# A graph kernel's loading stage and first node stage, written as one stage without engine loops

## The reference

```python
x_ij = jnp.concatenate([x[src], x[dst]], axis=1)
m_ij = jax.nn.relu(x_ij @ W.T + b)            # W is 512 x 1024
out = jax.ops.segment_sum(m_ij, src, num_segments=1250)
...
# second layer: attention, scores from h = x @ W1.T per head
e_src = einsum('ehd,hd->eh', h[src], a_src);  e_dst = einsum('ehd,hd->eh', h[dst], a_dst)
e = leaky_relu(e_src + e_dst, 0.2) * (1.0 + et_emb[edge_type]) * edge_weight[:, None]
```

## Time and profile before

| | |
|---|---|
| median of 3 runs | 1908.78 us (1907.65 to 1910.08) |
| the profiled execution | 1905.63 us, of which 1903.9 us are the span from first to last instruction |
| PE busy | 1596.2 us, 84% of the span, at a mean granted clock of 0.931 |
| DVE, ACT, POOL busy | 61%, 24%, 37% of the span |
| loading stage, from SP's first DMA to n0's first DVE instruction | 484.95 to 500.26 us |
| n0, to the first DVE instruction of e0 | 500.26 to 583.42 us |

### The profile page before, as it was taken

How to read it: one execution, slowest core, us unless ns; L and a number is a source line. 1 busy time by engine, 2 the same in 40 slices (tenths; PEclk the granted TensorE clock), 3 DMA queues, 4 the chain that set the end, 5 groups by cost and what they waited for, 6 DMA issues and landing times. The chain is left out here.

```text
span 1903.9 us, 26664 instructions
## 1 busy us (share of the span) xinstructions
PE 1596.2 (84%) x7565; PEld 956.2 (50%) x7566; DVE 1161.4 (61%) x2308; ACT 459.8 (24%) x875; POOL 700.1 (37%) x605
## 2 busy tenths in 40 slices
PE   6556939876698999998788379996698899999998
PEld 6524723335344555554555245553346445864486
DVE  7889959974375777775577766665865722122222
ACT  3101114424013555553344110000110111001100
POOL 0005878874475766640000547775330110000000
PEclk9988969998698999999799589999799999999999
DMA  0056841009315666680496447776005202330033
GB/s 26 1 215 247 286 118 12 3 2 358 133 39 155 209 188 187 187 143 34 176 361 236 133 121 210 210 209 158 2 1 173 70 0 106 138 111 0 1 138 137
DMA packets 76360, 249.16 MB, mean 131 GB/s; under 512 B 14901, under 2 KB 28582, under 8 KB 68346
## 3 DMA queue, kind: packets, MB, share of 16 engines
q1 hardware_dynamic: 38618, 147.08, 21.2%
q0 software_dynamic: 34592, 96.87, 19.0%
q10 hardware_dynamic: 3072, 4.20, 0.8%
HBM read 215.93 MB, written 32.00 MB: 130 GB/s over the span
## 5 line engine op out<-in xcount | busy, mean ns | idle before, releaser
L659 POOL DMA_INDIRECT tab_slots<-slot_words,slot_address x160 | 232.4, 1452 | 219.7 <-issue 209.0
L688 POOL DMA_INDIRECT e_rows<-tab_h,idx_h x176 | 178.7, 1015 | 290.5 <-POOLq L50 217.3
L1431 PE MATMUL dense_pY<-weights,dense_xT_block 128*128 128x512 f32 x640 | 284.0, 601 | 0.0
L1479 PE MATMUL dense_pY<-parts,dense_number 128*128 128x512 f32 x1000 | 237.2, 398 | 5.7 <-DMA dense_number<-tab_edges_to 5.7
L982 POOL DMA_INDIRECT e_rows<-tab_q,idx_q x192 | 182.0, 948 | 99.8 <-PE e_pS L1055 38.8
L1479 PEld LDWEIGHTS dense_pY<-parts,dense_number 128*128 128x128 f32 x1000 | 188.3, 189 | 53.3 <-DMA dense_number<-tab_edges_to 6.4
L782 PE MATMUL e_pS<-e_rows,e_onehot_ring 128*128 128x512 f32 x352 | 193.8, 641 | 21.7 <-DVE e_rows L758 18.6
L1431 PEld LDWEIGHTS dense_pY<-weights,dense_xT_block 128*128 128x128 f32 x640 | 121.5, 193 | 143.3 <-issue 143.3
L1055 PE MATMUL e_pS<-e_rows,e_onehot_f 128*128 128x512 f32 x384 | 181.6, 596 | 0.0
L867 PE MATMUL count_pA<-count_onehot_d,count_onehot_s 128*128 128x512 f16 (+1 forms) x576 | 132.4, 352 | 42.0 <-DVE count_onehot_d L850 40.9
L758 DVE TENSOR_TENSOR e_rows<-e_rows,e_pW 128x1024 f32<-128x1024 f32 x88 | 107.3, 1220 | 68.6 <-DMA e_rows<-tab_h,idx_h 68.5
(11 more groups left out here) (310 smaller groups left out, 2393.5 us busy)
## 6 DMA issues: line engine op xcount, KB each, us to landing
basis_piece<-in_L_gnn_basis_pieces SPq DMA_DIRECT2D x32, 2048.0 KB, 7.5
dense_number<-tab_edges_from SPq DMA_DIRECT2D x20, 1280.0 KB, 5.4
tab_edges_from<-counts_turned SPq DMA_DIRECT2D x10, 1280.0 KB
tab_edges_to<-counts_total SPq DMA_DIRECT2D x10, 640.0 KB
dense_number<-tab_edges_to SPq DMA_DIRECT2D x10, 640.0 KB, 4.3
tab_w<-basis_wout ACTq DMA_DIRECT2D x128, 32.0 KB
weights<-tab_w SPq DMA_DIRECT2D x4, 1024.0 KB, 6.3
weights<-in_L_gnn_W_T SPq DMA_DIRECT2D x3, 1024.0 KB
```

What stands on the lines that cost most here:

```text
L659: pool.indirect_dma_start(self.table, bass.IndirectOffsetOnAxis(self.address[:, t:t + 1], 0), self.words[:, t, :], None).then_inc(self.pla ...
L688: pool.indirect_dma_start(self.rows[:, q, s, :], None, self.table, bass.IndirectOffsetOnAxis(self.idx[:, j * 2 + s:j * 2 + s + 1], 0)).the ...
L1431: ins = self.nc.tensor.matmul(self.banks.at(g), self.xt[:, b % 2, c, :], weights[:, c, :], start=c == 0, stop=c == 3)
L1479: ins = self.nc.tensor.matmul(self.banks.at(self.first + b), self.number[:, b % 2, r * NB + k, :], self.parts[r][n][:, k, :], start=k == 0 ...
```

## The change

The two stages become one function, `first_nodes`, with one Block and one barrier at its end, and its blocks written out one after the other. PE turns X directly, without DVE's copy into `x_block`; `pT` gets two buffers. The score matmuls stand on PE after the multiplication of block 6. ACT writes P's high half by a cast to fp32r, and DVE only adds the bias and subtracts. SP loads the bias vector first, and waits before a store only for ACT's copy of Q. POOL zeroes `acc` and starts the factor when the slots are unpacked. The old score and loading code and `take_x` are removed; other uses of `node_stage` stay as they are.

```diff
+def first_nodes(nc, name, C, X, weights, vec, vectors, biases_in, p_parts, q_table, table, slots, slot_fields, loc, fields,
+                a_heads_in, score_in, score_w, wt, acc, factor):
...
+        xt, q_out = sb("xT_block", [P, 2, 4, P], F32), sb("q_out", [P, 2, D], F32)
+        biased = sb("biased", [P, 2, D], F32)
+        pt, py = ps("pT", [P, 2, 4, P], F32), ps("pY", [P, 2, 2, D], F32)
...
+        @block.sync
+        def _(sp):
+            sp.dma_start(vec[:, 0, :], vectors[0].partition_broadcast(P)).then_inc(bias_in, 16)
+            table.read_back(sp, flat(slots[:, :, :]), slots_read)
+            sp.dma_start(flat(a_heads[:, :, :]), a_heads_in).then_inc(raw_in, 16)
+            sp.dma_start(raw[:, :, :], score_in.rearrange("(c p) i -> p c i", p=P)).then_inc(raw_in, 16)
+            for k in range(1, len(vectors)):
+                sp.dma_start(vec[:, k, :], vectors[k].partition_broadcast(P)).then_inc(biases_in, 16)
+            for b in range(NB):
+                sp.wait_ge(q_ready, b + 1)
+                sp.dma_start(q_table[b * P:(b + 1) * P, :], q_out[:, b % 2, :]).then_inc(stored[b % 2], 16)
+            for k in range(2):
+                sp.wait_ge(stored[k], NB // 2 * 16)
+
+        @block.gpsimd
+        def _(pool):
+            nc.gpsimd.memset(acc[:, :, :], 0.0)
+            pool.wait_ge(unpacked, 1)
+            factor.compute(pool)
+
+        @block.vector
+        def _(v):
+            link = chain(v, s_dve)
+            nc.vector.memset(wt[:, :, H:H + 1], 1.0)
+            v.wait_ge(slots_read, 16)
+            unpack(link, nc, slot_fields, itmp, loc, fields)
+            v.sem_inc(unpacked, 1)
+
+            def add_bias(b):
+                v.wait_ge(multiplied, b + 1)
+                wait(v, low_out, b - 1)
+                nc.vector.tensor_tensor(biased[:, b % 2, :], py[:, b % 2, 0, :], vec[:, 0, :], ALU.add
+                                        ).then_inc(bias_added, 1)
+
+            def take_low(b):
+                v.wait_ge(high_out, b + 1)
+                v.wait_ge(bias_added, b + 1)
+                nc.vector.tensor_tensor(p_parts[1][:, b, :], biased[:, b % 2, :], p_parts[0][:, b, :].bitcast(F32),
+                                        ALU.subtract).then_inc(low_out, 1)
+
+            v.wait_ge(bias_in, 16)
+            for b in range(NB):
+                add_bias(b)
+                if b:
+                    take_low(b - 1)
+            take_low(NB - 1)
+
+        @block.scalar
+        def _(act):
+            def copy_x(b):
+                act.wait_ge(turned, b + 1)
+                wait(act, multiplied, b - 1)
+                nc.scalar.copy(xt[:, b % 2, :, :], pt[:, b % 2, :, :]).then_inc(copied, 1)
+
+            def finish(b):
+                act.wait_ge(multiplied, b + 1)
+                if b >= 2:
+                    act.wait_ge(stored[b % 2], b // 2 * 16)
+                nc.scalar.copy(q_out[:, b % 2, :], py[:, b % 2, 1, :]).then_inc(q_ready, 1)
+                act.wait_ge(bias_added, b + 1)
+                nc.scalar.copy(p_parts[0][:, b, :], biased[:, b % 2, :]).then_inc(high_out, 1)
+
+            for b in range(NB + 1):
+                if b < NB:
+                    copy_x(b)
+                if b:
+                    finish(b - 1)
+            act.wait_ge(score_made, 1)
+            nc.scalar.copy(score_w[:, :, :], pW[:, :, :])
+
+        @block.tensor
+        def _(pe):
+            def turn(b):
+                wait(pe, copied, b - 1)
+                for c in range(4):
+                    ins = nc.tensor.transpose(pt[:, b % 2, c, :], X[:, b, c * P:(c + 1) * P], C.f("ident"))
+                ins.then_inc(turned, 1)
+
+            def multiply(b):
+                pe.wait_ge(copied, b + 1)
+                wait(pe, bias_added, b - 1)
+                wait(pe, q_ready, b - 1)
+                for w in range(2):
+                    for c in range(4):
+                        ins = nc.tensor.matmul(py[:, b % 2, w, :], xt[:, b % 2, c, :], weights[w][:, c, :],
+                                               start=c == 0, stop=c == 3)
+                ins.then_inc(multiplied, 1)
+
+            turn(0)
+            for b in range(NB):
+                if b + 1 < NB:
+                    turn(b + 1)
+                multiply(b)
+                if b == 6:
+                    pe.wait_ge(raw_in, 32)
+                    for ic in range(4):
+                        for oc in range(4):
+                            ins = nc.tensor.matmul(pW[:, ic, :], raw[:, oc, ic * P:(ic + 1) * P], a_heads[:, oc, :],
+                                                   start=oc == 0, stop=oc == 3)
+                    ins.then_inc(score_made, 1)
...
-            @block.vector
-            def _(v):
-                link = chain(v, s_dve)
-                link(nc.vector.memset(acc[:, :, :], 0.0))
-                link(nc.vector.memset(wt[:, :, H:H + 1], 1.0))
...
-            node_stage(nc, "n0", X, C.f("ident"), take_x, 0,
-                       [(W[0], "bias_split", (V["L0_gnn_b"], p_parts)), (W[1], "table", None)], False,
...
+            first_nodes(nc, "n0", C, X, W[0:2], vec, [ins[v] for v in VECS], vecs_in, p_parts, tab["q"], table, slots,
...
```

More of the change, by code:

```diff
@@ L1336, in compute @@
                 link(nc.gpsimd.tensor_tensor(out[:, :, :], out[:, :, :], self.part[:, :, :], ALU.add))
+def first_nodes(nc, name, C, X, weights, vec, vectors, biases_in, p_parts, q_table, table, slots, slot_fields, loc, fields,
+                a_heads_in, score_in, score_w, wt, acc, factor):
+    FR = F32R
+    with ExitStack() as ctx:
+        sb = lambda n, s, d: ctx.enter_context(nc.sbuf_tensor(f"{name}_{n}", s, d))
+        ps = lambda n, s, d: ctx.enter_context(nc.psum_tensor(f"{name}_{n}", s, d))
+        sem = stage_semaphores(nc, ctx, name)
+        itmp = sb("unpack_tmp", [P, 2, SLOTS], I32)
+        raw, a_heads = sb("score_raw", [P, 4, D], F32), sb("a_by_head", [P, 4, 2 * H], F32)
+        xt, q_out = sb("xT_block", [P, 2, 4, P], F32), sb("q_out", [P, 2, D], F32)
+        biased = sb("biased", [P, 2, D], F32)
+        pt, py = ps("pT", [P, 2, 4, P], F32), ps("pY", [P, 2, 2, D], F32)
+        pW = ps("pScoreW", [P, 4, 2 * H], F32)
+        slots_read, raw_in, bias_in = sem("slots_read"), sem("raw_in"), sem("bias_in")
+        turned, copied, multiplied = sem("turned"), sem("copied"), sem("multiplied")
+        bias_added, high_out, low_out, q_ready = sem("bias_added"), sem("high_out"), sem("low_out"), sem("q_ready")
+        score_made, unpacked, s_dve = sem("score_made"), sem("unpacked"), sem("unpack_chain")
+        stored = [sem(f"stored{k}") for k in range(2)]
+        factor.begin(ctx, sem)
+        block = ctx.enter_context(nc.Block())
+        @block.sync
[87 more added lines that the diff above has]
+                    ins.then_inc(score_made, 1)
@@ L2234, in rows_of @@
         def rows_of(tile, b):
             return flat(tile[:, bass.ds(b, 1), :])
-        def take_x(link, v, normal, b, x):
-            link.take_wait()
-            return nc.vector.tensor_copy(x, rows_of(X, b))
         until_weights = ExitStack()
@@ L2245, in gnn @@
                        for n in ("high", "low")]
-            node_stage(nc, "n0", X, C.f("ident"), take_x, 0,
-                       [(W[0], "bias_split", (V["L0_gnn_b"], p_parts)), (W[1], "table", None)], False,
-                       [None, tab["q"]],
-                       beside=EdgeFactor(nc, "factor", ins["L1_gnn_et_emb"], types[:, :],
-                                         weight, factor))
+            first_nodes(nc, "n0", C, X, W[0:2], vec, [ins[v] for v in VECS], vecs_in, p_parts, tab["q"], table, slots,
+                        packed_dst, loc["dst"],
+                        [(idx["h"][:, :], SH1, 2047), (src_block[:, :], SH1 + 7, 15), (src_lo[:, :], SH1, P - 1),
+                         (types[:, :], SH2, 7)],
+                        ins["L1_gnn_a_heads"], ins["L1_gnn_W"], score_w, wt, acc,
+                        EdgeFactor(nc, "factor", ins["L1_gnn_et_emb"], types[:, :], weight, factor))
             edge_convolution(nc, "e0", C, identb, p_parts, tab["q"], idx["q"], loc["src"], pairs["src"], acc)
```

## The result

The changed kernel takes 1894.01 us (median of 6 executions, 1892.36 to 1898.88) against 1908.66 us for the kernel before (median of 6): a ratio of 0.9929, 95% interval 0.9918 to 0.994. The forecast for the median was 1894.6 us. The profiled execution took 1894.13 us, with a span of 1892.3 us.

What follows compares the result with a forecast made beforehand. PE was taken to bound n0's middle, leaving savings only before its first multiplication and behind its last. −14.92 − 0.96 + 3.28 − 1.61 = −14.2 us, from 1908.78 to a median of 1894.6 us, range 1890 to 1899.

Steps and rivals of the forecast that it cites:

- Start of PE: Behind `store_counts`: first transposes move from 500.75 to 485.83, skipping the loading stage's wait, matmuls and barrier; −14.92 us.
- late-start rival: At the stage's start: PE begins only at 488.5, losing 2.7 us of the gain; 1897.3 us, chance 0.10.
- Transposes to first multiplication: Ahead of block 0: both transpose groups run without waiting for ACT's copy, 1.8 us instead of 2.76; −0.96 us.
- Ten blocks: n0's middle: the same 160 matmuls and transposes at the same pace, 74.56 us, so no change.
- Engine loops, DVE's copy and masking worth 0: In n0's blocks: removing these saves nothing, since PE was busy without a gap, 7 us per block.
- Score matmuls: Behind block 6: 32 matmuls now stand inside PE's busy stretch; +3.28 us, upper bound 7.01.
- rival of a lower clock: In the score matmuls: PE's clock falls and they take up to 7.01 us; +3.7, 1898.3 us, chance 0.05.
- End of the stage: Last matmul to e0: store waits only for ACT's copy, so the tail falls from 5.35 to 3.74; −1.61 us.
- POOL: Stage start: clearing `acc` takes 8.8 us (bounds 4.33 and 13.0); factor ends 559.3, before the stage; costs nothing.
- Slower rival: Before block 2: POOL's memset beyond 14.3 us stalls DVE, then PE; chance 0.04 for 14 to 32 us, 0.03 longer.
- Clock kept into e0: At e0's start: PE's shorter pause keeps the clock up, halving 4.3 us; −2.15, 1892.4 us, chance 0.12.

Runs made afterwards that it cites:

- one `pT`: The changed kernel with a single buffer for the transposes instead of two; 1895.0 us against 1907.47 for the kernel before.
- masking on DVE: The changed kernel with DVE again making P's high half, both halves right behind the bias addition; 1893.74 us, ratio 0.9919 to the kernel before.
- memset four times: The changed kernel with POOL's memset of the accumulator done four times in a row; 1899.63 us against 1907.47 for the kernel before.
- memset later: Loading merged into the old looped node stage, with POOL's memset moved behind the wait for unpacked slots; 1904.35 us against 1909.72 for the kernel before.
- the score twice: The changed kernel with the 32 score matmuls done twice behind block 6; 1900.55 us against 1907.47 for the kernel before.

## Why the prediction was right, step by step

The time came 0.6 us under the forecast, and the stage's saving was 15.48 us where the sum was 14.2. The 1.3 us between these are 0.8 at the start of PE, 0.4 in the ten blocks and 0.2 at the end, less 0.2 in the score matmuls. That the whole time comes so close is partly chance: single executions scatter by more than 6 us in either kernel, and the profiled one, forecast at 1891.4, took 1894.13 because it came 3.55 us later to the stage.

- **Start of PE: right, under-sized.** PE was ready 0.04 us behind SP's DMA, not 0.88, the delay taken from DVE's first row. The late-start rival did not come.
- **Transposes to first multiplication: right** (1.76 us for 1.8); one `pT` gives the 0.91 back.
- **Ten blocks at no change: right.** Without the score matmuls they took 77.62 − 3.49 = 74.13 us for 74.56; the first started at 0.50 of the clock, as the sum had it, and the 0.4 us are its scatter (8.79 us for 9.25).
- **Engine loops, DVE's copy and masking worth 0: right for the kernel before, not for a merged stage.** With ScalarE's cast undone nothing changed. But the step asked only whether the work is covered by PE's 7 us per block, by DVE's time without POOL beside it; with what POOL held off, the copy of X was only 0.5 us early at the closest in the kernel before, and in the merged stage with a later memset it came late in six blocks. Ahead of the first block there is no such cover, and POOL's new memset would have held the copy for 4.4 us. With the loops and the copy kept, the merge gave half of the gain.
- **Score matmuls: right, 3.49 us for 3.28.** The rival of a lower clock is met in some executions: of eight profiles with the 32 matmuls between two blocks, five kept the clock and three lost it (masking on DVE, memset four times, memset later). Its price lay mostly in the block behind them (1.7 us in the first of these), not in the matmuls. What decides between the two stays open.
- **End of the stage: right.** 1.78 us saved for 1.61; the old wait put back costs 1.5. The last low half ended at 570.03, 2.1 us behind the last matmul, and nothing waited for it.
- **POOL: mis-sized, without effect.** The memset took 4.37 us, not 8.8: the lower bound, DVE's own time, came out, and the price by POOL's sums was wrong. The factor still ended (at 560.94) 72.4 us behind SP's first DMA, close to the 74.4 that the forecast's 559.3 means, since the unpacking waited for the slots until 492.44 and POOL then for its own DMA (496.19 to 502.99, 6.8 us instead of 3.27). That is 7.6 us ahead of the last store's issue.
- **Slower rival: right in its mechanism, far from its condition.** It needs 14.3 us and the memset took 4.37. With four memsets PE stood about as long as the threshold gives (3 us for 3.3), but by two errors that offset each other: behind the last memset only 2.1 us of unpacking were left for the 3.6 of the sum, and between the bias addition and PE stood ACT's cast and copy, 1.2 us that the sum leaves out. One memset of that length was not run. By the rival's own rule a memset of 36 us would give 1916 us and not 1909.
- **Clock kept into e0: did not come.** The clock was 1.00 until 571 and 0.50 from 573 on, with PE's pause down to 4.05 us, and behind the stage both kernels need the same time.

## What to carry to other kernels

Where one engine is busy without a gap through a stage's middle, look at what stands ahead of its first instruction and behind its last: here 18.56 and 5.35 us held all of the gain. Work that must run on that engine but that nothing in the stage waits for (the score matmuls) is best put into a gap that remains: under the landing of the last store it cost 2.6 us less than between two blocks. Before moving a long instruction to POOL, list which DVE instructions start beside it and who waits for them; price the wait by the whole POOL instruction, and ask it again for the first block, where no other work covers it.

## What the runs showed of the hardware that was not expected

- POOL clears 128x5120 in 4.37 us, as fast as DVE (4.33), though by its sums (2.61 us for 1408 elements) as many elements would be some 9 us, an estimate.
- The subtraction of the low half (two operands in SBUF) took 2.66 us instead of 0.68 in the first timeline of the result. It began at 543.57 and ended at 546.23, 0.55 us behind the POOL sum that ran from 542.51 to 545.68; POOL's next instruction in turn took 0.97 us instead of 0.66. The Trainium skill (SBUF — State Buffer, "Who interferes with whom") has the rule: a VectorE instruction with two SBUF inputs contends with a GpSimd instruction that reads SBUF, so moving the masking to ScalarE doesn't take DVE out of the contention. The trace agrees.
- PE's granted clock fell under a row of 16-column matmuls with no gap between them (1.00 in 543 to 544, 0.50 in 546 to 547 in the kernel with the score twice), and it was still low for the wide matmuls that followed (9.30 us for 7.03). With half as many it fell in three profiles of eight.
